# Second attention of a two-layer transformer kernel: maximum tiles cut into single heads, three per step at one place, and projections in two pieces

## The reference, cut to what matters

```python
q = apply_rope((x @ q_w.T + q_b).reshape(B, S, H, Dh).transpose(0, 2, 1, 3))   # B=2, S=1024, H=16, Dh=16
k = apply_rope((x @ k_w.T + k_b).reshape(...)); v = (x @ v_w.T + v_b).reshape(...)
attn = jnp.einsum('bhqd,bhkd->bhqk', q, k) * Dh ** (-0.5)
probs = jax.nn.softmax(attn, axis=-1)
out = jnp.einsum('bhqk,bhkd->bhqd', probs, v)
return out.transpose(0, 2, 1, 3).reshape(B, S, D) @ out_w.T + out_b
```

## Time and profile before

| what | value |
|---|---|
| median of the runs | 837.85 us (835.2 to 838.43) |
| profiled execution, own time | 833.41 us |
| its span, first to last instruction | 831.6 us |
| outside the span | 1.8 us |
| PE busy | 747.8 us, 90% |
| DVE busy | 558.0 us, 67% |
| ACT busy | 424.7 us, 51% |
| POOL busy | 273.6 us, 33% |
| first `values` matmul of the second attention | 520.41 us |
| last `values` matmul, start | 817.94 us |

### The profile page before, as it was taken

How to read it: one execution, slowest core, us unless ns; L and a number is a source line. 1 busy time by engine, 2 the same in 40 slices (tenths; PEclk the granted TensorE clock), 3 DMA queues, 4 the chain that set the end, 5 groups by cost and what they waited for, 6 DMA issues and landing times.

```text
span 831.6 us, 11322 instructions
## 1 busy us (share of the span) xinstructions
PE 747.8 (90%) x4298; PEld 454.2 (55%) x4298; DVE 558.0 (67%) x872; ACT 424.7 (51%) x557; POOL 273.6 (33%) x271
## 2 busy tenths in 40 slices
PE   4777799999977999789999998999999998999897
PEld 3666688886666888556556555333334333333324
DVE  4775446545565546978988987677777777777605
ACT  2434133435444332211211213888887888888793
POOL 0378888635242543311111112021231223122310
PEclk9898899999989999989999999999999999999999
DMA  6137100101000247442201112144333334433211
GB/s 231 52 100 260 52 1 1 50 2 57 1 1 0 76 153 253 146 135 101 95 8 51 52 52 66 57 136 128 109 104 129 126 108 132 145 130 97 70 39 61
DMA packets 25705, 74.16 MB, mean 89 GB/s; under 512 B 4604, under 2 KB 5980, under 8 KB 24692
## 3 DMA queue, kind: packets, MB, share of 16 engines
q1 hardware_dynamic: 21124, 65.37, 23.8%
q0 software_dynamic: 3808, 7.60, 3.1%
q10 hardware_dynamic: 720, 0.48, 0.2%
HBM read 54.54 MB, written 23.06 MB: 93 GB/s over the span
## 4 chain that ended last, share of the span: by engine, by line
PE 62%; DVE 16%; issue 7%; ACT 7%; POOL 5%; DMA 2%; ACTq 0%; DVEq 0%; POOLq 0%
PE PS L684 19%; PE PS L916 12%; PE PS L690 8%; PE PS L902 7%; PE PS L885 6%; DVE mx L1179 5%; PE PS L873 4%; ACT P L1365 4%; PE PS L715 3%; DVE mx L1187 2%; DVE XC L1002 1%; DMA BKV<-in_bkv 1%; POOL ek L1416 1%; PE PS L767 1%; DVE bst L985 1%
## 5 line engine op out<-in xcount | busy, mean ns | idle before, releaser
L1365 ACT ACTIVATE P<-PS 128x1024 f32<-128x1024 f32 x256 | 248.7, 1024 | 39.1 <-PE PS L902 36.8
L1187 DVE TENSOR_REDUCE mx<-PS 128x1 f32<-128x512 f32 x284 | 183.0, 686 | 68.4 <-PE PS L885 67.1
L1452 POOL TENSOR_TENSOR hl<-sg,hh 128x512 fp32r<-128x512 f32 x64 | 82.1, 1285 | 204.0 <-ACT hh L1338 204.0
L1179 DVE TENSOR_REDUCE mx<-PS 128x2 f32<-128x1024 f32 x114 | 134.8, 1220 | 17.3 <-PE PS L873 16.8
L916 PE MATMUL PS<-P,VV 128*32 128x512 f32 x1024 | 137.3, 608 | 0.5
L902 PE MATMUL PS<-QS,KS 64*128 64x512 f32 x512 | 110.9, 453 | 8.0 <-ACT P L1365 7.3
L1338 ACT ACTIVATE hh<-sg 128x512 fp32r<-128x512 f32 x64 | 40.4, 630 | 131.8 <-DVE sg L1121 89.1
L902 PEld LDWEIGHTS PS<-QS,KS 64*128 64x128 f32 x512 | 47.9, 184 | 83.4 <-ACT P L1365 74.5
L885 PE MATMUL PS<-KM,QM 64*128 64x512 f32 x284 | 67.1, 466 | 6.8 <-DVE mx L1187 6.3
L885 PEld LDWEIGHTS PS<-KM,QM 64*128 64x128 f32 x284 | 27.4, 184 | 77.6 <-DVE mx L1187 64.2
L873 PE MATMUL PS<-KM,QM 64*128 64x512 f32 x228 | 52.5, 486 | 14.5 <-DVE mx L1179 9.6
(11 more groups left out here) (195 smaller groups left out, 1424.2 us busy)
## 6 DMA issues: line engine op xcount, KB each, us to landing
QM<-scr_q SPq DMA_DIRECT2D x16, 512.0 KB, 4.3
KM<-scr_k SPq DMA_DIRECT2D x16, 512.0 KB, 5.3
QS<-scr_q SPq DMA_DIRECT2D x16, 512.0 KB, 4.5
KS<-scr_k SPq DMA_DIRECT2D x16, 512.0 KB, 6.0
scr_q<-spl SPq DMA_DIRECT2D x24, 256.0 KB, 3.6
scr_k<-spl SPq DMA_DIRECT2D x24, 256.0 KB, 3.3
scr_o<-OE POOLq DMA_DIRECT2D x14, 256.0 KB, 3.0
stg<-in_tern SPq DMA_DIRECT2D x3, 1024.0 KB, 4.9
```

Source lines behind the costliest of these rows:

```text
L1179: e.tensor_reduce(mx[p % 2][:, :, qt, half], PS[:, b:b + 2, :], AX.X, ALU.max).then_inc(q["mx"], 2)
L1187: e.tensor_reduce(mx[p % 2][:, h, qt, half:half + 1], bank[b], AX.X, ALU.max).then_inc(q["mx"], 1)
L1365: e.activation(P[s % 4][:, half * 1024:(half + 1) * 1024], PS[:, b:b + 2, :].rearrange("p b n -> p (b n)"), ACT.Exp).then_inc(q["ex"], 1)
L1452: e.tensor_tensor(hl[f % 4][:, :], sg[f % 3][:, :], r32(hh[f % 4][:, :]), ALU.subtract).then_inc(q["hl"], 1)
```

## The change

The two heads of a maximum tile become pieces of their own, `max_half(p, u, h, b)`: one matmul, one bank, one reduction. After `scores(s, 1)`, and only there, up to three halves are put per step (`HALVES`, `MOST`). In a step that holds a piece of a projection, none is put. A projection is cut into its two token tiles (r = 0, 1), three matmuls each, that stand in successive steps and share one bank, held from the first to the second; DVE adds once, at r = 1. The projection of group 2 begins at step 116 (`LATE`) at the earliest. The early tiles stay as they are.

```diff
-EARLY, EVERY = 114, 1.72
+EARLY, HALVES, MOST, LATE = 114, 3, 3, 116
...
+    def half_tile(ring):
+        k = next(halves, None)
+        if k is None:
+            return False
+        n, h = divmod(k, 2)
+        put("max_half", *divmod(n, 16), h, ring.next())
+        if h == 1:
+            tile_done(n, ring)
+        return True
+
+    def tile_done(n, ring):
         p, u = divmod(n, 16)
-        if ring is ps:
-            put("max", p, u, ring.pair())
-        else:
-            put("max_each", p, u, ring.next(), ring.next())
         if u == 15:
             put("max_join", p)
...
         if (u == 2 and p > 0) or n == 16 * NP - 1:
             r = p - 1 if u == 2 else p
-            put("max_rows", r, tb.next())
+            put("max_rows", r, ring.next())
...
-                    for n in range(4):
-                        later(s + 3 + n, "project", piece[1], n)
+                    first = s + 3 if piece[1] < 2 else max(s + 3, LATE)
+                    for i in range(8):
+                        later(first + i, "project", piece[1], i // 2, i % 2)
+            elif piece[0] == "project":
+                if piece[3] == 0:
+                    held = mxr.next()
+                put(*piece, held)
...
             put("scores", s, 0, st.pair())
-            spend(0.5)
...
-            spend(1.1)
         if live:
             put("scores", s, 1, st.pair())
-            spend(0.6)
+            due += HALVES
+            for _ in range(MOST):
+                if due >= 1 and all(piece[0] != "project" for piece in plan.get(s, [])) and half_tile(mxr):
+                    due -= 1
...
-            def max_each(p, u, *banks):
+            def max_half(p, u, h, b):
                 qt, half = divmod(u, 2)
-                if u == 0:
+                if u == 0 and h == 0:
                     e.wait_ge(d[f"km{p % 2}"], slot_value(p))
                     e.wait_ge(d[f"qm{p % 2}"], slot_value(p))
-                for b in banks:
-                    claim(b)
-                for h, b in enumerate(banks):
-                    hr = slice(64 * h, 64 * h + 64)
-                    e.matmul(...).then_inc(q["mt"], 1)
-                    freed[b] = q["mx"], 32 * p + 2 * u + h + 1
+                claim(b)
+                hr = slice(64 * h, 64 * h + 64)
+                e.matmul(...).then_inc(q["mt"], 1)
+                freed[b] = q["mx"], 32 * p + 2 * u + h + 1
```

More of the change, by code:

```diff
@@ L260, in work_order, with tile @@
     done = {}
[L262 to L266, removed]
+    def tile(ring):
+        n = next(tiles)
+        put("max", *divmod(n, 16), ring.pair())
+        tile_done(n, ring)
[6 more added lines that the diff above has]
+        if h == 1:
+            tile_done(n, ring)
+        return True
+    def tile_done(n, ring):
         p, u = divmod(n, 16)
-        if ring is ps:
-            put("max", p, u, ring.pair())
-        else:
-            put("max_each", p, u, ring.next(), ring.next())
         if u == 15:
@@ L297, in early @@
         def early():
-            tile(ps, ps)
+            tile(ps)
         yield from ln1_pair(2, 3)
@@ L327, in later @@
         plan.setdefault(s, []).append(piece)
+    halves = iter(range(2 * next(tiles), 32 * NP))
     due = 0.0
[L331 to L336, removed]
     s, loaded = 0, 2
@@ L647, in recip, with project @@
                     recip_out(e, p)
-            def project(g, n, b):
-                if g == 1:
+            def project(g, n, r, b):
+                if g == 1 and r == 1:
                     e.wait_ge(q["pjx"], 4 * g + n + 1)
@@ L874, in max_tile @@
                 freed[b] = freed[b + 1] = q["mx"], 32 * p + 2 * u + 2
-            def max_each(p, u, *banks):
+            def max_half(p, u, h, b):
                 qt, half = divmod(u, 2)
-                if u == 0:
+                if u == 0 and h == 0:
                     e.wait_ge(d[f"km{p % 2}"], slot_value(p))
                     e.wait_ge(d[f"qm{p % 2}"], slot_value(p))
-                for b in banks:
-                    claim(b)
-                for h, b in enumerate(banks):
-                    hr = slice(64 * h, 64 * h + 64)
-                    e.matmul(bank[b], QM[p % 2][hr, qt * 128:(qt + 1) * 128], KM[p % 2][hr, chunk(half)], start=True, stop=True).then_inc(q["mt"], 1)
-                    freed[b] = q["mx"], 32 * p + 2 * u + h + 1
+                claim(b)
+                hr = slice(64 * h, 64 * h + 64)
+                e.matmul(bank[b], QM[p % 2][hr, qt * 128:(qt + 1) * 128], KM[p % 2][hr, chunk(half)], start=True, stop=True).then_inc(q["mt"], 1)
+                freed[b] = q["mx"], 32 * p + 2 * u + h + 1
             def max_rows(p, b):
@@ L918, in values, with project @@
                 i.then_inc(q["pv"], 1)
-            def project(g, n, b):
+            def project(g, n, r, b):
                 i, f = g % 2, g % 2
[L922 to L928, removed]
+                ts = slice((2 * n + r) * 128, (2 * n + r + 1) * 128)
+                if r == 0:
+                    claim(b)
+                    e.wait_ge(q["gl"], g + 1)
+                o = two_tiles(bank[b], r, ((OH[i][:, ts], WOH[:, f, :]), (OH[i][:, ts], WOL[:, f, :]), (OL[i][:, ts], WOH[:, f, :])), True, True)
+                if r == 1:
+                    o.then_inc(q["pj"], 1)
+                    freed[b] = q["pjx"], 4 * g + n + 1
             def last(banks):
@@ L953, in _ @@
             parts = {f.__name__: f for f in (start, ln_turn, tern_scale, kv_in, kv_out, q0, att_z, att_m, att_b, prep_down, prep_ug,
-                                             gate, up, down, ffn_end, qk, v, max_each, max_rows, scores, values, project, last)}
+                                             gate, up, down, ffn_end, qk, v, max_half, max_rows, scores, values, project, last)}
             parts["max"] = max_tile
@@ L1179, in max_tile, with max_half @@
                 e.tensor_reduce(mx[p % 2][:, :, qt, half], PS[:, b:b + 2, :], AX.X, ALU.max).then_inc(q["mx"], 2)
-            def max_each(p, u, *banks):
-                if u == 0 and p > 1:
+            def max_half(p, u, h, b):
+                if u == 0 and h == 0 and p > 1:
                     e.wait_ge(q["mc"], p - 1)
                 qt, half = divmod(u, 2)
-                for h, b in enumerate(banks):
-                    e.wait_ge(q["mt"], 32 * p + 2 * u + h + 1)
-                    e.tensor_reduce(mx[p % 2][:, h, qt, half:half + 1], bank[b], AX.X, ALU.max).then_inc(q["mx"], 1)
+                e.wait_ge(q["mt"], 32 * p + 2 * u + h + 1)
+                e.tensor_reduce(mx[p % 2][:, h, qt, half:half + 1], bank[b], AX.X, ALU.max).then_inc(q["mx"], 1)
             def max_join(p):
@@ L1211, in group, with project @@
                 e.scalar_tensor_tensor(OL[i][:, :], NUM[i][:, :], col("vb1", f), r32(OH[i][:, :]), ALU.add, ALU.subtract).then_inc(q["gl"], 1)
-            def project(g, n, b):
+            def project(g, n, r, b):
+                if r == 0:
+                    return
                 bt, f = divmod(g, 2)
@@ L1238, in _ @@
             parts = {f.__name__: f for f in (start, ln_stats, ln_norm, ln_turn, bias, w0l, signs, tern_scale, tern_cut, half, scales, kv_in, kv_sums, q0, att_z,
-                                             att_m, att_b, gate, up, ffn_end, prep_down, prep_ug, qk, qk_split, max_each, max_join, recip, group, project, last)}
+                                             att_m, att_b, gate, up, ffn_end, prep_down, prep_ug, qk, qk_split, max_half, max_join, recip, group, project, last)}
             parts["max"] = max_tile
```

## The result

| | before | after |
|---|---|---|
| median | 838.43 us (5 runs, 835.2 to 839.03) | 843.56 us (5 runs, 842.03 to 846.88) |
| ratio of the runs | | 1.0074, 95% interval 1.0045 to 1.0103 |
| profiled execution, its span | 833.41, 831.6 us | 843.42, 841.6 us |
| first to last values of the second attention | 297.5 us | 308.0 us |

I forecast no measurable change (835.4 us, range 827 to 847). The kernel became slower, clear of the interval. The profiled executions differ by 10.0 us, and the stage from first to last values differs by 10.5: all of it is in the second attention.

What follows compares the result with a forecast made beforehand. The order on PE and its waits in the second attention were taken as the bound. Terms to step 111 summed to 257.3 us against 257.4, the rest gained 2.4: 837.85 - 2.5 = 835.4 us, range 827 to 847.

Steps and rivals of the forecast that it cites:

- the term "group": Cost of the copies OH on ACT and OL on DVE at three groups: 4.1 us, from 2 to 8.
- POOL's and SP's transfers keep their steps: Transfers in the second attention stay at their steps; `out` to `recip` has 13 us for a way of about 9.
- the sign itself: At the groups, ACT waiting for POOL over 2 us at one of them would show the forecast wrong.
- Rival 3: OH's wait for NUM through memory sets the pace at three groups: +2 us against the forecast, 838; chance 0.05.
- Rival 1: The third head's bank is free in time, leaving PE's 2.12 us per step: -10 us, 827.5; chance 0.30.
- rival 2: The first two single heads on PE do not run together, 2.35 us per step: +12, 850; chance 0.22.
- the sum: Second attention: 257.3 us against 257.4 to step 111's values, then a gain of 2.4; total -2.5 us.
- 2.18 per step: Plain step with three single heads, paced by the loop through the banks: 2.12 and about 2.23 us in turn.
- halves of projections: Projection steps with three fewer matmuls on PE: 2.39 us each instead of 2.75.
- the turn of the maxima: `max_rows` makes one piece wait for a same-step reduction, 8 x 0.9 us; the last tile in step 110, 1.9.
- bare steps: Steps after step 111's values without heads or projection: 1.98 us each, four of them 7.9.
- The release of one wait: Delay from DVE's reduction to a single head on PE: 0.04 us, with 0.14 as bound, giving 2.23 per step.

Runs made afterwards that it cites:

- e1: The changed kernel with the three groups two steps later; 831.11 us, ratio 0.9938 to the kernel before.
- e8: The changed kernel with the groups one step later; 836.86 us, ratio 0.9984 to the kernel before.
- e2: The changed kernel with the reciprocals one step earlier, groups at the same steps; 838.91 us, ratio 1.0019 to the kernel before.
- e9: e6 with the groups one step later still; ratio 1.0163 to the kernel before.
- e6: e1 with `max_rows` in a slot of its own, ahead of the next step's heads; 825.7 us, ratio 0.9853 to the kernel before.
- e5: The kernel before with the groups two steps later, as a control; ratio 1.0031 to the kernel before.
- e3: The kernel before with the reciprocals one step later, groups at their old steps; 846.74 us, ratio 1.0116 to it.

## Why the prediction was wrong

**The step that failed is the term "group"**: 4.1 us, with bounds of 2 to 8. Moving the groups two steps later (e1) takes 13.4 us off the stage, and OH and OL cost something in e1 as well. Three parts of the term were wrong.
- The waits. I took 0, 1.2 and 0.5 us; they were 2.91, 2.61 and 1.66. I had read the way from OE's start to NUM's end (8.95 us) as fixed and let only ACT come earlier. It was 12.05, 10.49 and 9.55, and ACT came 0.6 us earlier at most. The 8.95 was also not the way of one pair: it runs from the next pair's OE to the product of the four before it, tied only by POOL's order.
- The sentence "POOL's and SP's transfers keep their steps". `recip`, `load_s` and `group` keep them in the list, but not in time: which of two engines reaches its piece first decided the order of scr_r and the load of QS and KS, and in group 1 the gap was 0.6 us either way. I did not ask what DVE does ahead of the reciprocal. The load of QM and KM does not keep its step at all: it follows the sixteenth maximum tile of a pair, and for pair 12 that moved from step 49 to step 41, the very step whose `out` sends the scr_o that stands ahead of group 0's product on POOL. That load was issued 2.2 us ahead of scr_o there (610.94 against 613.14), which then took the 2.3 us more.
- The clock. I priced a stall at its own length. e8, e2 and the changed kernel have 2.3, 4.4 and 7.2 us of waits and 6.8, 10.2 and 17.0 us at the lower level, and their stages are 5.2, 8.5 and 13.4 us longer than e1's. Waits at their length and the lower clock at 0.4 of its length give 5.0, 8.5 and 14.0. So the fall costs nearly as much again as the wait. The 0.4 is fitted to these three, and of the lower clock 3.4 us in e8 and in e2 stand behind the last maximum tile and not behind OH. For the long waits of e9 the same sum is too high: 20.2 + 0.4 x 27.3 = 31 over e6, measured 24.5. The clock of 1.00 in the earlier trace rows holds for a stretch without such waits.

The prediction had named the sign itself: it is wrong "if ACT waits for POOL more than 2 us at one group". ACT did at two, for 2.91 and 2.61 us.

Rival 3 had the place right and the size wrong by over six times: +2 us at a chance of 0.05, where the changed kernel is 13.0 us above the forecast stage (308.0 against 295.0). It, too, held the way fixed. Rival 1 and rival 2 are refuted by the chain: steps alternate, and the first two heads run together (0.23 for both at 597.59).

**What was right.** Without that wait the sum holds. It gave a stage of 297.5 - 2.5 = 295.0 us; e1 measures 294.6. That agreement is partly luck, as 4.1 us of groups stood in it. But its parts agree one by one: 2.18 per step, halves of projections at 2.41 (2.39 forecast), the turn of the maxima about 0.9 dearer than its neighbours (3.18 against 2.24), bare steps at 3.96 for two, as forecast. The release of one wait is 0.04 (543.07 in the rows beside e6) and not 0.14, which decided between 2.18 and 2.23. One picture in it was off at no cost: the third head does not stand alone. When its bank is free it starts together with the first score (both at 593.29 in PE's timeline), and the second score is alone instead. The gain over the kernel before is 0.6% once the groups have room, less than half of what the order allows: e6 takes another 0.9%, from the slot of `max_rows` that I had priced at 8 x 0.9 + 1.9 us and not questioned.

What stays open: what a wait of about 1 us does to the clock (behind 1.35 in e6 and 1.02 in e8 it fell, behind 1.23 in e8 it did not), why the last maximum tile is followed by a fall in e2, e5 and e8 and not in e1, and, but for the estimates above, how much of e3 and of e5's loss has which cause.

## What to carry to other kernels

When an order changes, list every wait whose other end is a way through memory. Don't take the length of that way as fixed, and count its slack in microseconds, not in steps; then give it room first, since this one number turned 0.7% slower into 0.6% faster. Ask, too, what the way really joins: here a product waited for another pair's sums only because one engine works in order. A small transfer that races a large one by half a microsecond is a coin that any reordering can turn: look at which engine issues which, and when it really gets there. And a deadline moved later in a shared in-order list can land behind the next item that waits: two steps helped here, while in e9 one more than in e6 cost 3%.

## What the runs showed of the hardware

- Three waits of ACT, 1.66 to 2.91 us, left PE idle for 3.38, 3.06 and 2.13 us of an otherwise full stage, and each was followed by 3.4 or 6.8 us at the lower clock (0.91 and 0.83 over 20 us); at the third, the last maximum tile stops PE again meanwhile. At that level values take 1.86 us instead of 1.00. In these short waits the fall cost about as much as the wait. That the array's clock is gated to one of two levels by how busy the array was shortly before is what the Trainium skill ("TensorE: Matmul & The Clock Gate", Part 1) says; by that, the trace agrees.
- A transfer of 8 KB lands in 1.7 us (median of 14, before the change), or in 5.0 (after it) when 1 MB has been issued 0.3 to 0.6 us ahead on another queue. The Trainium skill ("DMA: Bandwidth & Descriptors", Queues, rings and completion order) says that a DMA engine takes turns between its queues packet by packet. From that alone I would have expected the small transfer to be held up little. The measurement decides: 3.3 us more.
- Three DVE reductions back to back take 1.89 us where one takes 0.69. A 64-row matmul behind one satisfied wait starts beside its neighbour of the other half, whether that is a single head (0.23 us for both) or a score.
